# Joining the weight-times-value sets of two chunks in the fused attention stage

## Chip, cores and metric

One of the eight cores of a Trainium2 chip runs the whole kernel. The metric is the device time of one execution in microseconds, as the median of several runs. Its tensor engine is called PE here, VectorE DVE, ScalarE ACT, GpSimd POOL and SyncE SP, as in the profile.

## What is computed

The block is one transformer layer: causal attention with 16 heads of 16 columns over 8 sequences of 1024 rows, and a mixture of 8 experts, of which each row uses two, both with a residual and layer norms.

```python
q, k, v = (heads(einsum('oi,bsi->bso', W, layernorm(x))) for W in (Wq, Wk, Wv))
score = einsum('bhnd,bhmd->bhnm', q, k) / sqrt(16)        # -inf above the diagonal
out = einsum('bhnm,bhmd->bhnd', softmax(score), v)
x = x + layernorm(einsum('oi,bsi->bso', Wo, out))
logits = layernorm(x) @ router_weight.T + router_bias      # top 2 of 8 experts
x = x + layernorm(experts(layernorm(x)))
```

## The kernel before

Three stages follow one another: the fused attention stage (`attention_layer`, up to about 1412 us), the experts, and a closing sum. The change touches only the first, in which each engine runs its own unrolled list of instructions over `SLOTS`, and semaphores tie the lists together. The order within an engine is written out by hand.

**Scores and weights.** Four heads make a quad; there are 32 quads. A head has 12 *maximum* chunks (`MAXC`, here m0 to m11; widths 128, 256, 384, 512, then four times a 512 followed by 128, 256, 384, 512): PE computes scores into one of three banks `ps_s` (`max_scores`, L834) and DVE reduces them to row maxima (`maximum`, L485 and L488). The maxima pass ACT (`high`, L707) and POOL (L409), PE turns them over (`max_rows`, L841) into the third bank of `ps_s`, DVE copies them out (`mrow`, L499), and a DMA issued by POOL (L414) puts them beside the queries. m8 of the next head must wait for that copy (`c == ROWS_AT + 1`). Six heads later PE computes the scores again, now less their maximum, in 12 *exponential* chunks per quad (`EXPC`, widths 512, 384, 256, 128, four times 512, then 512, 384, 256, 128) for each of the four heads, into one of three banks `ps_e` (`exp_scores`, L853). ACT turns them into `pw` (`exponential`, L700), which holds four chunks; POOL cuts the chunks on the diagonal (L403); and `weigh` (L872) multiplies the four heads' weights with their values side by side in four column groups of 32 of the array, into one bank `ps_o`, which ACT empties twice per quad (`head_out`, L714).

**Slots.** Slot `g` stands for one exponential chunk of one quad (`NE` = 12 slots in a quad; the text numbers them 0 to 11 by `g % 12`). It has four sub-steps `s`; each holds one maximum chunk and the exponential scores of head `s` of chunk `g + 1`. The maximum of a head takes three slots, m0 to m3, m4 to m7, m8 to m11, starting at slots 0, 3, 6 and 9. `max_rows` falls into sub-step 3 of slots 1, 4, 7 and 10. At the end of each slot stands `weigh(g - 1)`. The maximum scores run from slot -18 (`BEGIN`) to 365, the exponentials for slots 0 to 383.

**Pieces between.** For each of 32 pairs of row tiles the projections for a later sequence (starts `A_AT`) and the output projection, layer norms and router of an earlier one (starts `C_AT`) are cut into pieces, each due at an offset from its start: `turn_over` (L885), `q_or_k` (L904, four steps for m = 0 and four for m = 1), `values` (L919), `project` (L944), `turn_rows` (L965), `route` (L976), `rank` (L988, L991), all through one shared bank `ps_w`: each first waits until the last user of the bank has been read (`bank_free`). Readers are on ACT `first_part` (L724), `second_part` (L730), the copies to `xn_t` (L751), `vout` (L767), `y` (L784), `h_t` (L806) and the normalisations to `xn`, `y`, `h` (L776, L789, L798); on DVE `remainder` (L508), the statistics (L593, L600, L607, L641, L650), `logits`, `top`, `top_at` (L655, L613, L619), `choose` and `place`; on POOL `third` (L394), the small row statistics (L438 to L444), the residual sum (L452) and the indirect stores of rows for the experts (L462, 128 of them at slots `S_AT`). SP issues loads and stores. The last four pairs (`LATE`) and the last groups run in slots from 384 on, without scores beside them.

## Time and profile before

| | us |
|---|---|
| median of three runs (lowest, highest) | 2316.2 (2313.4, 2321.1) |
| the profiled execution | 2312.5 |
| its span, first to last instruction | 2310.7 |
| busy in the span: PE, DVE, ACT, POOL | 2003.9, 1687.1, 1132.6, 975.5 |
| steady part of the fused stage | 200 to 1280 |
| first and last weight-times-value set | 137.8, 1320.9 |
| last indirect store for the experts begins about | 1411 |

Busy times overlap from engine to engine. A matmul's end in the profile is modelled, so neighbouring matmuls overlap on paper; the distance from start to start is what one of them keeps PE from the next. "Idle before, releaser" is the time for which an engine stood still and what ended it.

### The profile page before, as it was taken

To read this page: it belongs to the slowest core of one execution; us is meant where nothing else is said; L and a number is where in the kernel's file an instruction comes from. 1 tells how busy PE (TensorE), PEld (TensorE's weight loads), DVE (VectorE), ACT (ScalarE), POOL (GpSimd) and SP (SyncE) were. 2 spreads that over 40 slices of the span, in tenths; PEclk is the share of its full clock that TensorE was granted. 3 is DMA by queue.
4 is the path that set the end of the run, shared out by engine and by line. 5 is a ranking of instruction groups with operands and counts; after the bars stand their busy time and mean duration, and the time that the engine had idled before them with its cause. 6 is when DMAs were issued, how large, how long until landed. Compare 5 with 4: busy or idle time off the path is not lost. (4 is left out here: it accounts for less than half of the span.)

```text
span 2310.7 us, 51852 instructions
## 1 busy us (share of the span) xinstructions
PE 2003.9 (87%) x13629; PEld 1307.3 (57%) x13630; DVE 1687.1 (73%) x5978; ACT 1132.6 (49%) x2647; POOL 975.5 (42%) x1583
## 2 busy tenths in 40 slices
PE   5499999999999999999989842999999999999960
PEld 4243444444444444444333331998898888888950
DVE  2487768787888888888868232777777777777768
ACT  3156667777777777777766720222222222222220
POOL 4122334445646465555544553333333333333326
PEclk9789999999999999999999955999999999999985
DMA  5926575767666666768584223887787778778766
GB/s 156 183 63 145 125 167 150 183 153 178 146 167 140 163 145 168 152 154 172 111 215 95 97 82 136 238 242 233 238 239 236 236 233 235 232 238 238 236 193 237
DMA packets 259627, 412.94 MB, mean 179 GB/s; under 512 B 37136, under 2 KB 194960, under 8 KB 253200
## 3 DMA queue, kind: packets, MB, share of 16 engines
q1 hardware_dynamic: 220432, 367.20, 58.6%
q0 software_dynamic: 29824, 35.54, 7.4%
q10 hardware_dynamic: 9216, 8.39, 1.1%
q8 instruction: 66, 1.08, 0.2%
q14 instruction: 89, 0.73, 0.1%
HBM read 288.30 MB, written 122.14 MB: 178 GB/s over the span
## 5 line engine op out<-in xcount | busy, mean ns | idle before, releaser
L700 ACT ACTIVATE pw<-ps_e 128x512 f32<-128x512 f32 (+3 forms) x1536 | 688.7, 493 | 310.2 <-PE ps_e L853 301.7
L1244 PE MATMUL ps_g<-x_t,w_gu 128*128 128x128 f32 x4384 | 541.7, 277 | 28.1 <-ACT x_t L1175 21.9
L834 PE MATMUL ps_s<-ks,qs 96*128 96x512 bf16 (+3 forms) x1536 | 492.9, 336 | 67.0 <-DVE mrow L499 34.1
L1244 PEld LDWEIGHTS ps_g<-x_t,w_gu 128*128 128x128 f32 x4384 | 515.2, 192 | 59.2 <-issue 49.1
L485 DVE CUSTOM_DVE_ANT_0 summed<-ps_s,c 128x128 bf16<-128x128 f32 (+3 forms) x1024 | 480.3, 482 | 83.2 <-PE ps_s L834 79.4
L853 PE MATMUL ps_e<-qs,ks 98*128 98x512 bf16 (+3 forms) x1536 | 487.1, 331 | 3.2 <-ACT pw L700 3.0
L488 DVE TENSOR_REDUCE cmax<-ps_s 128x1 f32<-128x512 f32 x512 | 351.5, 686 | 142.7 <-PE ps_s L834 139.9
L834 PEld LDWEIGHTS ps_s<-ks,qs 96*128 96x128 bf16 x1536 | 152.8, 101 | 405.0 <-issue 120.2
L872 PE MATMUL ps_o<-pw,vs 128*32 128x512 f32 (+3 forms) x3072 | 332.7, 506 | 4.9 <-ACT ot L714 2.8
L1196 ACT ACTIVATE d_y<-biased,weight 128x256 f32<-128x256 f32 x136 | 69.1, 508 | 490.3 <-DVE biased L1155 490.3
L403 POOL TENSOR_SCALAR_AFFINE_SELECT pw<-pw 128x512 f32<-128x512 f32 x256 | 162.1, 633 | 310.9 <-ACT pw L700 310.8
L1210 POOL DMA_INDIRECT acc<-d_y,place_now x136 | 214.8, 1580 | 120.5 <-issue 74.5
L1273 PE MATMUL ps_y<-space,act_h 128*128 x1088 | 258.1, 380 | 0.8 <-DVE act_h L1148 0.8
L1136 DVE TENSOR_SCALAR gate<-ps_g,space 128x128 f32<-128x128 f32 x548 | 154.4, 345 | 105.4 <-issue 94.1
L853 PEld LDWEIGHTS ps_e<-qs,ks 98*128 98x128 bf16 x1536 | 149.8, 98 | 110.2 <-ACT pw L700 19.9
L1273 PEld LDWEIGHTS ps_y<-space,act_h 128*128 128x128 f32 x1088 | 196.1, 190 | 22.6 <-issue 1.5
L1203 POOL TENSOR_TENSOR place_now<-place,c 128x1 int32<-128x1 int32 x136 | 24.9, 183 | 430.9 <-ACT d_y L1196 430.5
L1141 DVE TENSOR_SCALAR up<-ps_g,space 128x128 f32<-128x128 f32 x548 | 154.3, 344 | 9.0 <-PE ps_g L1244 0.2
L462 POOL DMA_INDIRECT xs<-c_h,slot_i x128 | 131.5, 1027 | 33.2 <-issue 32.6
L872 PEld LDWEIGHTS ps_o<-pw,vs 128*32 128x32 f32 x3072 | 60.9, 108 | 121.9 <-issue 80.1
L414 POOL DMA_DIRECT2D qs<-mrow x128 | 81.5, 637 | 109.6 <-DVE mrow L499 105.3
L1179 ACT ACTIVATE sig<-gate 128x512 f32<-128x512 f32 x137 | 86.3, 630 | 79.2 <-DVE gate L1136 79.2
(136 smaller groups left out, 2289.6 us busy)
## 6 DMA issues: line engine op xcount, KB each, us to landing
w_gu<-in_gate_up SPq DMA_DIRECT2D x138, 1024.0 KB, 5.0
qk_parts<-space SPq DMA_DIRECT2D x128, 192.0 KB, 7.2
qs<-qk_parts SPq DMA_DIRECT2D x192, 128.0 KB, 7.3
ks<-qk_parts SPq DMA_DIRECT2D x192, 128.0 KB, 7.8
d_xin<-xs SPq DMA_DIRECT2D x139, 130.5 KB, 2.5
v_aug<-space SPq DMA_DIRECT2D x32, 512.0 KB, 7.4
vs<-v_aug SPq DMA_DIRECT2D x32, 512.0 KB, 11.6
o_t<-ot SPq DMA_DIRECT2D x64, 256.0 KB, 2.8
```

Of the source, the lines that this page charges most:

```text
L403: pool.affine_select(diagonal, diagonal, [[0, 4], [1, P]], ALU.is_ge, 0.0, base=0, channel_multiplier=-1).then_inc(cut_done, 1)
L485: dve.tensor_tensor_reduce(summed[:, m % RJ, 0:w], ps_s[:, m % RS, 0:w], after[:, HALF - w:HALF], 1.0, LOWEST, ALU.add, ALU.max, dst).then ...
L488: dve.reduce_max(dst, ps_s[:, m % RS, 0:w], AX.X).then_inc(s_cmax, 1)
L700: act.activation(pw[:, n % RP, 0:w], ps_e[:, n % RE, 0:w], ACT.Exp, scale=SCALE).then_inc(e_done, 1)
L834: pe.matmul(ps_s[:, m % RS, 0:w], qs[0:ROWS, slot, i * P:(i + 1) * P], ks[0:ROWS, slot, k0:k0 + w], start=True, stop=True).then_inc(s_scor ...
L853: pe.matmul(ps_e[:, n % RE, 0:w], ks[0:ROWS_M, slot, j * P:(j + 1) * P], qs[0:ROWS_M, slot, q0:q0 + w], start=True, stop=True).then_inc(e_ ...
L872: last = pe.matmul(ps_o[s * QUAD:(s + 1) * QUAD, at:at + w], vs[:, u, j, s], pw[:, (g * 4 + s) % RP, 0:w], start=(j == 0), stop=(c + 1 in ...
L1136: last = dve.tensor_scalar(gate[:, u, m], ps_g[:, u, 0, m], b_gu[:, bass.ds(e, 1), m], LIMIT, ALU.add, ALU.min)
L1141: last = dve.tensor_scalar(up[:, m], ps_g[:, u, 1, m], b_gu[:, bass.ds(e, 1), KI + m], LIMIT + 1, ALU.add, ALU.min)
L1210: pool.indirect_dma_start(out=acc, out_offset=bass.IndirectOffsetOnAxis(place_now[:, u:u + 1], 0), in_=y[:, u], in_offset=None, compute_op ...
L1244: last = pe.matmul(ps_g[:, u, half, m % KI], w_gu[:, u, k, m * P:(m + 1) * P], x_t[:, u, k], start=(k == 0), stop=(k == KT - 1))
L1273: last = pe.matmul(ps_y[:, u, 0:D], act_h[:, u, m], w_dn[:, bass.ds(e, 1), m], start=(m == 0), stop=(m == KI - 1))
```

## The change

The call of `weigh` leaves the odd slots; in each even slot `g` the sets of chunks `g - 2` and `g - 1` run one behind the other. The large PE pieces go to the odd slots: `turn_over` to slot 7, `q_or_k` m = 0 to 9, m = 1 to 11 with its last step at the head of slot 0, both `values` to 1, both halves of `project` to 3, both of `route` to 5; `turn_rows` goes to slot 4 and `rank` to slot 10. So `A_AT` moves by one slot, the readers on ACT, DVE and POOL get new offsets, `turn_rows`, `route` and what follows them run eleven slots later for the pairs before `LATE`, and the indirect stores are spread anew. No operation is added or dropped. The blocks below follow in the order SP, POOL, DVE, ACT, PE.

```diff
-    A_AT = [BEGIN - 18 + 3 * a for a in range(EARLY)] + [BEGIN - 5, BEGIN + 2] + [NE * (a - 6) - 4 for a in range(6, PAIRS)]
+    A_AT = [BEGIN - 18 + 3 * a for a in range(EARLY)] + [BEGIN - 6, BEGIN + 1] + [NE * (a - 6) - 5 for a in range(6, PAIRS)]
...
-    EVEN = [30 + d for turn in range(0, 4 * NE, NE) for d in (turn, turn + 6, turn + 7, turn + 9, turn + 10)]
+    EVEN = [34 + turn + d for turn in range(0, 3 * NE, NE) for d in (0, 3, 5, 5, 7, 9)]
...
-    MOMENTS = [(r, k) for slot, k, r in sorted((C_AT[r] + 3 + 6 * k, k, r) for r in range(PAIRS) for k in range(2))]
+    MOMENTS = [(r, k) for slot, k, r in sorted((C_AT[r] + 3 + (7 if r < LATE else 6) * k, k, r) for r in range(PAIRS) for k in range(2))]
...
+    def rows_due(steady, late, slot):
+        return [r for r, start in enumerate(C_AT) if start + (steady if r < LATE else late) == slot]
...
+    NEVER = SLOTS.stop + NE * QUADS
...
-                for a in pairs_due(-1, -9, g):
+                for a in pairs_due(-1, -8, g):
...
-                for k, offset in enumerate((5, 10)):
-                    for r in due(C_AT, offset, g):
+                for k, offsets in enumerate(((4, 4), (11, 10))):
+                    for r in rows_due(*offsets, g):
...
-                for r in due(C_AT, 7, g):
+                for r in due(C_AT, 6, g):
...
-                for a in due(A_AT, 6, g):
+                for a in pairs_due(7, 8, g):
...
-                for a in due(A_AT, 3, g):
+                for a in due(A_AT, 4, g):
...
-                        for n in groups_due(19, 19, g):
-                            choose(n, 0)
+                        for n in groups_due(31, 20, g):
+                            choose(n, 2)
                     if s == 1:
-                        for n in groups_due(22, 19, g):
-                            choose(n, 1)
-                        for n in groups_due(27, 21, g):
-                            place(n, 0)
...
+                        for a in due(A_AT, 3, g):
+                            remainder(a, 0)
...
-                        for r in due(C_AT, 9, g):
+                        for r in rows_due(10, 9, g):
...
-                        for r in due(C_AT, 17, g):
-                            half, t = r // PER % 2, r % PER * 2
-                            dve.wait_ge(c_lg, r + 1)
-                            for c in range(t, t + 2):
-                                last = dve.max(top[:, half, c], logits[:, half, c])
-                            last.then_inc(c_top, 1)
-                        for r in due(C_AT, 18, g):
+                        for r in rows_due(30, 18, g):
...
                     if s == 2:
-                        for n in groups_due(25, 19, g):
-                            choose(n, 2)
-                        for n in groups_due(27, 21, g):
+                        for n in groups_due(30, 19, g):
+                            choose(n, 0)
+                        for n in groups_due(32, 21, g):
...
-                        for n in groups_due(28, 21, g):
+                        for n in groups_due(33, 21, g):
...
-                        for n in groups_due(29, 21, g):
...
                     if s == 3:
-                        for a in due(A_AT, 2, g):
-                            remainder(a, 0)
-                        for a in due(A_AT, 4, g):
+                        for a in due(A_AT, 5, g):
...
-                        for k, offset in enumerate((4, 9)):
-                            for r in due(C_AT, offset, g):
+                        for k, offsets in enumerate(((3, 3), (10, 9))):
+                            for r in rows_due(*offsets, g):
...
-                        for r in due(C_AT, 16, g):
+                        for r in rows_due(26, 16, g):
...
+                        for r in rows_due(27, 17, g):
+                            half, t = r // PER % 2, r % PER * 2
+                            dve.wait_ge(c_lg, r + 1)
+                            for c in range(t, t + 2):
+                                last = dve.max(top[:, half, c], logits[:, half, c])
+                            last.then_inc(c_top, 1)
+                        for n in groups_due(30, 19, g):
+                            choose(n, 1)
+                        for n in groups_due(31, 20, g):
+                            place(n, 0)
...
                     if s == 2:
-                        for a in due(A_AT, 0, g):
-                            act.wait_ge(a_tps, a + 1)
-                            if a >= 2:
-                                act.wait_ge(a_v, a - 1)
-                            bank = ps_e[:, 0] if a < EARLY else ps_w[:]
-                            act.activation(xn_t[:, a % 2], bank.rearrange("p (k t) -> p k t", k=KT), ACT.Copy).then_inc(a_xt, 1)
-                        for a in due(A_AT, 2, g):
-                            first_part(a, 0)
-                        for a in due(A_AT, 3, g):
-                            second_part(a, 0)
-                        for a in due(A_AT, 4, g):
-                            first_part(a, 1)
-                        for a in due(A_AT, 5, g):
-                            second_part(a, 1)
-                        for a in due(A_AT, 6, g):
+                        for a in due(A_AT, 7, g):
...
-                        for a in pairs_due(-2, -10, g):
+                        for a in due(A_AT, 0, g):
+                            act.wait_ge(a_tps, a + 1)
+                            if a >= 2:
+                                act.wait_ge(a_v, a - 1)
+                            bank = ps_e[:, 0] if a < EARLY else ps_w[:]
+                            act.activation(xn_t[:, a % 2], bank.rearrange("p (k t) -> p k t", k=KT), ACT.Copy).then_inc(a_xt, 1)
+                        for a in due(A_AT, 6, g):
+                            second_part(a, 1)
+                        for a in due(A_AT, 3, g):
+                            second_part(a, 0)
+                        for a in due(A_AT, 5, g):
+                            first_part(a, 1)
+                        for a in pairs_due(-2, -9, g):
...
-                        for r in due(C_AT, 1, g):
-                            bank = ps_w[:] if r < LATE else ps_s[:, r % 2]
-                            act.wait_ge(c_w, r + 1)
-                            if r >= 2:
-                                act.wait_ge(c_x1, r - 1)
-                            act.activation(y[:, r % 2], w_view(bank), ACT.Copy).then_inc(c_raw, 1)
-                        for r in due(C_AT, 6, g):
+                        for r in due(C_AT, 5, g):
...
-                        for r in due(C_AT, 11, g):
+                        for r in rows_due(15, 11, g):
...
-                        for r in due(C_AT, 14, g):
+                        for r in rows_due(25, 14, g):
...
-                        for n in groups_due(20, 20, g):
+                        for n in groups_due(31, 20, g):
...
+                    if s == 3:
+                        for a in due(A_AT, 2, g):
+                            first_part(a, 0)
+                        for r in rows_due(0, 1, g):
+                            bank = ps_w[:] if r < LATE else ps_s[:, r % 2]
+                            act.wait_ge(c_w, r + 1)
+                            if r >= 2:
+                                act.wait_ge(c_x1, r - 1)
+                            act.activation(y[:, r % 2], w_view(bank), ACT.Copy).then_inc(c_raw, 1)
...
                     if s == 0:
-                        for n in groups_due(27, 20, g):
+                        for a in due(A_AT, 5, g):
+                            q_or_k(a, 1, (3,))
+                        for n in groups_due(NEVER, 20, g):
...
-                        for a in due(A_AT, 4, g):
-                            q_or_k(a, 1, (1,))
                     if s == 1:
...
-                        for a in due(A_AT, 1, g):
+                        for a in due(A_AT, 2, g):
...
+                        for a in due(A_AT, 4, g):
+                            q_or_k(a, 1, (0, 1))
+                        for a in due(A_AT, 6, g):
+                            values(a, 0)
+                        for r in due(C_AT, 0, g):
+                            project(r, 0)
+                        for r in rows_due(25, 14, g):
+                            turn_rows(r)
+                        for r in rows_due(26, 16, g):
+                            route(r, 0)
+                            route(r, 1)
+                    if s == 2:
...
-                            q_or_k(a, 1, (2, 3))
-                        for a in due(A_AT, 5, g):
-                            values(a, 0)
+                            q_or_k(a, 1, (2,))
...
-                            project(r, 0)
-                        for r in due(C_AT, 1, g):
...
-                        for r in due(C_AT, 14, g):
-                            turn_rows(r)
-                        for r in due(C_AT, 16, g):
-                            route(r, 1)
-                    if s == 2:
-                        for a in due(A_AT, 3, g):
-                            q_or_k(a, 1, (0,))
-                        for r in due(C_AT, 15, g):
-                            route(r, 0)
-                if 0 < g <= NE * QUADS:
-                    weigh(g - 1)
+                        for n in groups_due(31, NEVER, g):
+                            rank(n)
+                if g % 2 == 0:
+                    for chunk in (g - 2, g - 1):
+                        if 0 <= chunk < NE * QUADS:
+                            weigh(chunk)
```

## Rows read from the trace of the kernel before

**Rows 1.** The page, busy time, share of the span and instructions of PE.
```profile
PE 2003.9 (87%) x13629; PEld 1307.3 (57%) x13630; DVE 1687.1 (73%) x5978; ACT 1132.6 (49%) x2647; POOL 975.5 (42%) x1583
```
**Rows 2.** Windows, steady stretch: length, busy PE, PEld, DVE, ACT, POOL, clock, DMA, GB/s.
```profile
200.00:1280.00 1080.00, 1030.05 (x6837) 479.00 (x6837) 855.04 (x3158) 795.60 (x1920) 532.19 (x939) 0.99 0.66 154
```
**Rows 3.** Groups by shape, PE, 200 to 1280 us: busy, mean ns | idle before, releasers.
```profile
L834 PE MATMUL ps_s<-ks,qs 96*128 96x512 bf16 x687 | 262.6, 386 | 30.8 <-DVE mrow L499 22.0 <-DVE rmax L485 7.6 <-DVE cmax L488 1.1
...
L872 PE MATMUL ps_o<-pw,vs 128*32 128x512 f32 x1352 | 185.0, 620 | 1.9 <-ACT ot L714 1.3
...
L919 PE MATMUL ps_w<-space 128*128 128x256 f32 x192 | 53.1, 399 | 10.8 <-DVE space L508 10.8
...
L976 PE MATMUL ps_w<-w_r,h_t 128*128 128x8 f32 x200 | 25.8, 237 | 2.1 <-DVE base L548 2.1
```
**Rows 4.** Timeline of PE, slots 11 to 1: start, duration, instruction, count.
```profile
704.37 0.38 PE L834 MATMUL ps_s<-ks,qs 96*128 96x512 bf16 x1
704.59 0.38 PE L853 MATMUL ps_e<-qs,ks 98*128 98x512 bf16 x1
704.90 0.64 PE L872 MATMUL ps_o<-pw,vs 128*32 128x256 f32 x8
705.47 0.23 PE L834 MATMUL ps_s<-ks,qs 96*128 96x128 bf16 x1
...
708.08 0.43 PE L872 MATMUL ps_o<-pw,vs 128*32 128x128 f32 x8
708.44 0.39 PE L834 MATMUL ps_s<-ks,qs 96*128 96x512 bf16 x1
...
709.56 1.13 PE L919 MATMUL ps_w<-space 128*128 128x256 f32 x4 [0.45 <-DVE space L508]
```
**Rows 5.** Timeline of PE, last slots of the stage: two sets in one group.
```profile
1318.70 1.28 PE L872 MATMUL ps_o<-pw,vs 128*32 128x384 f32 x16
```
**Rows 6.** Timeline of all engines, slot 0: the chain ahead of the values.
```profile
707.44 0.33 PE L853 MATMUL ps_e<-qs,ks 98*128 98x384 bf16 x1
...
707.81 0.49 ACT L700 ACTIVATE pw<-ps_e 128x384 f32<-128x384 f32 x1 [0.71 <-PE ps_e L853]
...
708.19 0.59 ACT L724 ACTIVATE space<-ps_w 128x512 bf16<-128x512 f32 x1
...
708.82 0.69 DVE L508 TENSOR_TENSOR space<-ps_w,space 128x512 f32<-128x512 f32 x1
```
**Rows 7.** Windows, four us behind a long wait for mrow (columns as rows 2).
```profile
222.00:226.00 4.00, 4.00 (x16) 0.88 (x15) 2.02 (x8) 1.94 (x4) 1.21 (x4) 0.50 0.69 268
```
**Rows 8.** Timeline, transpose of the maxima and its copy, slot 1, then slot 7.
```profile
711.07 0.22 PE L841 MATMUL ps_s<-c,mpart 128*16 128x128 bf16 x1
...
711.56 0.20 DVE L499 COPY mrow<-ps_s 16x128 bf16<-16x128 bf16 x1
...
729.86 0.22 PE L841 MATMUL ps_s<-c,mpart 128*16 128x128 bf16 x1
730.25 0.20 DVE L499 COPY mrow<-ps_s 16x128 bf16<-16x128 bf16 x1
```
**Rows 9.** Timeline, slots 4 and 5: the copy and the m8 that waits for it.
```profile
721.57 0.21 DVE L499 COPY mrow<-ps_s 16x128 bf16<-16x128 bf16 x1 [0.62 <-DMA qs<-mrow]
...
721.93 0.38 PE L834 MATMUL ps_s<-ks,qs 96*128 96x512 bf16 x1 [0.55 <-DVE mrow L499]
```
**Rows 10.** Timeline of ACT, slot 3: two exponentials of 512 columns.
```profile
718.96 1.08 ACT L700 ACTIVATE pw<-ps_e 128x512 f32<-128x512 f32 x2 [0.42 <-PE ps_e L853]
```
**Rows 11.** Timeline of PE and DVE, slot 10 of a late quad: m4 and m7.
```profile
1111.02 0.39 PE L834 MATMUL ps_s<-ks,qs 96*128 96x512 bf16 x1
...
1111.45 0.69 DVE L488 TENSOR_REDUCE cmax<-ps_s 128x1 f32<-128x512 f32 x1
...
1112.19 0.28 PE L834 MATMUL ps_s<-ks,qs 96*128 96x256 bf16 x1 [0.25 <-DVE cmax L488]
```
**Rows 12.** Groups of POOL, 1371 to 1412 us.
```profile
L462 POOL DMA_INDIRECT xs<-c_h,slot_i x31 | 30.6, 987 | 9.6 <-issue 9.6
```

## The prediction

> **What bounds the kernel now.** The tensor engine (PE) leads over the span [rows 1]. I read next the table of stages: in the steady stretch of the fused stage, 200 to 1280 us, PE is busy 1030 of 1080 us at granted clock 0.99, VectorE (DVE) 855 and ScalarE (ACT) 796 [rows 2]. Then the PE groups by shape in the same stretch: the reader is to see how little PE idles. The maximum scores wait 30.8 us (22.0 of it for the copy of mrow), the values products 10.8, the weight-times-value sets 1.9, the router product 2.1 [rows 3]. So PE's own time counts there, and a change is worth what it takes from PE's queue less what it makes PE wait for. A chunk slot lasts about 3.1 us; I number the twelve slots of a quad 0 to 11, and the twelve maximum scores of a head m0 to m11. Last I read PE's timeline from start to start, since modelled ends overlap.
>
> **Part by part. 1, the sets joined.** Scores follow a 512-wide score after 0.22 us, a set only after 0.31: 0.09, here taken as 0.10, lies ahead of a set. A set of 256 columns holds PE 0.57 us, one of 128 columns 0.36: 0.21 per 128 columns and 0.15 that doesn't depend on width [rows 4]. Two sets back to back occur once in the trace, in the last slots: 384 and 256 columns, modelled 1.28 us together [rows 5]; apart they would take 0.21 x 3 + 0.15 and then 0.64 (the duration of the lone 256-column set), 1.42. So joining saves 0.14 behind one set and 0.10 ahead of the next, 0.245 per pair. The maximum scores end at slot 366 and PE is the bound until then: 183 pairs, **-45 us**. Lower bound: only the front gap, -18.
>
> The Trainium skill, "TensorE: Matmul & The Clock Gate", Part 3 (Packing small matmuls), says that a weight load overlaps running matmuls only when it goes to other row groups; the weights of both sets use all rows, so by it the second set could not start seamlessly and only the -18 would be left. The joined pair speaks against it [rows 5]; it is rival 4.
>
> **2, the values products.** They now start 0.45 us late by the record, 0.6 from start to start, because the remainder of the projection ends just before [rows 4, 6]. Afterwards the last query/key piece runs at the head of slot 0, and the four scores' rest (about 1.0), a weigh pair of 128+256 columns (0.9) and 0.5 of slot 1 lie between: 2.4 us. The chain it waits for: exponential 0.37 behind its matmul, 0.38 to the next activation, first part 0.6, remainder 0.7 [rows 6], started 0.43 late: 2.6. Left 0.24 of 0.62, 28 times: **-11** (0 to -17).
>
> **3, the waits for ot and base** [rows 3] get a slot more or a weigh pair in front: with the slack around them **-5**.
>
> **4, the mrow copy.** In slot 4 DVE waits for the DMA of the previous mrow, and m8 of the next slot waits for the copy; PE idles 22.0 us in all [rows 3]. The path of the DMA stays; what lies between on PE grows from a 128-column set to 384 columns in a pair (+0.4), and part 6's wait comes ahead of it. I take 13 of the 22. Around the longest of these waits the clock falls to half for a few us [rows 7]; four such places before 360 us cost about 2 us each; I give back 2: **-15** (0 to -30).
>
> **5, the same copy where no set covers it.** The mrow transpose is the last but one matmul of slots 1, 4, 7 and 10, and m8, first in the next slot, waits for the copy out of PSUM. Transpose to copy is 0.49 us in slot 1 and 0.39 in slot 7 [rows 8]; copy to m8, where nothing else holds PE, is 0.36 [rows 9]. Now a set always lies between. Afterwards the sets are in even slots, so behind slots 1 and 7 only one exponential score does: 0.15 + 0.11 and 0.15 + 0.22. PE waits 0.85 - 0.26 = 0.59 and 0.75 - 0.37 = 0.38: 0.97 a quad, 31 quads, **+30** (+15 if the copy comes quicker, +35). Queued behind m8 is everything of PE; DVE and ACT run dry meanwhile.
>
> **6, turning of rows.** project moves whole into slot 3, y's copy to slot 3 behind its last exponential and the small high part (0.2), and turn_rows of an earlier pair needs that PSUM bank in slot 4, sub-step 1. From project's end: exponential score 0.22, 0.37 to ACT [rows 6], 0.48 for the exponential (two in 1.08 us) [rows 10], 0.2, copy and signal 0.65: 1.9 us. PE has 1.16 of scores. Wait 0.75, 26 pairs: **+19** (+5 if ACT lets the copy pass sooner, +30 if it lags). The old place had a set and more than a slot between.
>
> **7, rank** moves to slot 10, sub-step 2, and needs the bank that the remainder in sub-step 1 reads, itself behind a first part at the end of slot 9: by the chain of part 2 about 1 us, for six groups, **+6**.
>
> **8, DVE's pace.** PE may be three maximum banks ahead. Where four maxima follow without other PE work, the fourth waits for the first. Trace of slot 10 in a late quad, without pieces: m4 issued at 1111.02, DVE starts it 0.43 later, needs 0.69, m7 goes at 1112.19 where PE was ready 0.4 earlier [rows 11]. Afterwards slots 2, 6, 8, 10 are without pieces in every quad. Slot 10: m3 (512 wide, DVE 0.6) now lies 0.33 ahead of m4, with no set between, so m4 ends at 1.4 and m7, wanted at 0.68, waits 0.8. Slot 2: m8 ends at 1.2, m11 wanted at 0.78: 0.4. Slot 6: m2 waits for m11 behind slot 5's 2.6 us of DVE work, 0.3. Sum 1.5. The trace's own small waits of this kind, 0.45 a quad in PE's start-to-start excess, go: +1.05, 30 quads, **+31** (0 if DVE runs no later than now, +50).
>
> **9, outside.** Head: the same pieces, values and vout one slot later; stores still at +9: +1 (-3 to +5). The last 18 slots, where ACT sets the pace with exponentials: wider breaks, +2. Tail: POOL's 31 indirect stores run to its end at 1.3 us each [rows 12]; what starts them is the last pair's chain, which gets pair 27's turning, router and y copy in front (about 2 us), and one more store stays behind it (1.3): +3. Together **+6** (-3 to +12). SP's queue keeps its order but for the input load, one slot later and not near a wait; POOL's third and row statistics move by a slot under its idle time. Both at nothing, +3 if DVE then waits for them.
>
> **Sum.** -45 - 11 - 5 - 15 + 30 + 19 + 6 + 31 + 6 = +16. The profiled execution took 2312.5 us (span 2310.7 and 1.8 around it), the median of three runs 3.7 more. 2312.5 + 16 = 2328.5; half of the 3.7 added, **2330**.
>
> **Rivals.** 1, not slower: DVE's pace does not bite. It stays ahead because PE's new waits (5, 6) let it catch up; then term 8 is zero and 6 falls by 5: 16 - 31 - 5 = -20, 2294 with the same half; with the lower bounds of 5 and 6 it reaches 2270. For it: DVE is busy only 79% [rows 2]. Against: the late wait came with DVE just as idle [rows 11]. It decides at the point where m4 is done within 0.7 us of its issue in slot 10. 2, the costs of 5 and 6 hold and half of 8: all cancels, 2309 to 2323. 3, slower by more: ACT starves in the joined sets. A pair of two 512-column sets holds PE 1.95 us, three banked exponentials last 1.45 [rows 10]; 0.5 and 0.4 of latency idle ACT. In slots 5 and 6 ACT's work is 5.5 us (eight exponentials, ot, the high part, h's two normalisations that move there) against PE's 5.8, so 0.6 is over, in 7 and 8 0.2: +24, 2354. Against it: the normalisations lie just ahead of the sets and count as bank. 4, the joined set does not start seamlessly: 27 of the 45 are lost, 2357.
>
> **Chances.** Forecast (2323 to 2345) 0.41, rival 1 0.30, rival 2 0.17, rival 3 0.07, rival 4 0.05. Measurement tells 0.3%, 7 us. Slower 0.41 + 0.07 + 0.05 = 0.53; same 0.17; faster 0.30. The range cuts the low third of rival 1 and the tops of 3 and 4: 2282 to 2352. Signs are mixed, so the forecast's own 2323 to 2345 stands beside it.
>
> **What would show it.** Right: weigh groups of 16 records whose time is 0.21 per 128 columns + 0.15 once; PE's wait for mrow above 22 us, at slots 2 and 8, with about 0.6 and 0.4 each; a PE wait for y's copy before turn_rows of 0.5 to 1; no 0.45 before the values; maximum scores in slots 2, 6, 10 waiting for cmax. Wrong: PE idle in the stretch not above the 45 us it has now, or DVE and ACT waiting for PE more while PE has no gaps (rival 1); ACT without waits and PE waiting for pw (rival 3); a joined group as long as two (rival 4). What would make the forecast wrong is above all the size of 8, an addition over several slots.

## The result, and the profile after

| | before | after |
|---|---|---|
| median of four runs each (lowest, highest) | 2314.8 (2310.1, 2321.1) | 2355.7 (2352.9, 2365.0) |
| span of the profiled execution | 2310.7 | 2355.7 |

The changed kernel is slower: ratio 1.0182, 95% interval 1.0144 to 1.022, some 41 us by the medians and 45 by the profiled spans. The forecast, 2330 with a range of 2282 to 2352, had the sign and 14 us of it. Among the experiments below only one run (3580.2 us, of before_light2) fell into a slower state; it is left out of that kernel's median.

The page's busy times of after (PE, its loads, DVE, ACT, POOL), and the row of the steady stretch, which answers to [rows 2]:

```profile
PE 2011.2 (85%) x13629; PEld 1331.0 (57%) x13630; DVE 1687.2 (72%) x5978; ACT 1132.4 (48%) x2647; POOL 972.4 (41%) x1583
...
200.00:1280.00 1080.00, 1001.97 (x6628) 486.16 (x6621) 825.14 (x3041) 770.50 (x1859) 513.14 (x912) 0.98 0.66 152
```

PE was busy for 1030 us of this stretch and is for 1002, 2.7% less; DVE and ACT, whose work per quad is unchanged, are busy for 3.5% and 3.2% less. So the same time holds some 3.3% less of the kernel's work, and PE's gain can't be read from this row: its busy time per quad did not fall, since it holds part of the waits and the slower clock. The distances from start to start below show it. The groups of PE by shape, 200 to 1280 us (busy, mean ns | idle before, releasers), answer to [rows 3]:

```profile
L839 PE MATMUL ps_s<-ks,qs 96*128 96x512 bf16 x663 | 255.4, 387 | 40.6 <-DVE mrow L504 18.1 <-DVE rmax L490 16.3 <-DVE cmax L493 6.0
L858 PE MATMUL ps_e<-qs,ks 98*128 98x512 bf16 x660 | 243.9, 384 | 1.3 <-ACT pw L704 1.2
L877 PE MATMUL ps_o<-pw,vs 128*32 128x512 f32 x1324 | 171.5, 621 | 0.0
...
L924 PE MATMUL ps_w<-space 128*128 128x256 f32 x192 | 51.8, 392 | 5.5 <-DVE space L513 4.0
```

The maximum scores wait 40.6 us in place of 30.8, and DVE's maxima (L490, L493) hold most of what is new. Two waits did not exist before, for y's copy ahead of `turn_rows` (L970) and for the remainder ahead of `rank` (L993); a view of PE's waits in the same stretch (waited for: us in total, times, longest) lists them:

```profile
PE ps_s L839 <- DVE mrow L504: 18.1, 61, 1.5
...
PE ps_w L970 <- ACT c_y L817: 13.4, 24, 0.6
PE ps_s L839 <- DVE cmax L493: 10.0, 51, 0.3
PE ps_w L993 <- DVE space L513: 7.4, 4, 1.8
PE ps_w L924 <- DVE space L513: 4.0, 4, 1.0
```

Mrow's wait fell from 22.0 to 18.1 us, but it came in 21 places and comes in 61.

**Where the 45 us lie.** From the start of the first maximum score of a slot to the same of a later slot, in both timelines:

| stretch | before | after | difference |
|---|---|---|---|
| start to slot 0 | 131.9 | 137.5 | +5.6 |
| quads 0 and 1 | 71.8 | 72.8 | +1.0 |
| quads 2 to 5 | 160.2 | 149.9 | -10.3 |
| quads 6 to 23 | 678.4 | 707.0 | +28.6 |
| quads 24 to 29 | 221.8 | 235.0 | +13.3 |
| slot 360 to the last set | 56.9 | 62.7 | +5.7 |
| from there to the end | 989.8 | 990.8 | +1.0 |

Windows over the same stretches give the granted clock (third number from the end). Before, then after:

```profile
203.70:363.90 160.20, 150.16 (x928) 65.61 (x924) 115.31 (x399) 108.12 (x262) 54.64 (x104) 0.93 0.64 147
363.90:1042.30 678.40, 658.89 (x4433) 321.02 (x4430) 550.34 (x2046) 517.43 (x1248) 360.91 (x635) 1.00 0.68 160
1042.30:1264.00 221.70, 202.17 (x1360) 84.30 (x1356) 172.70 (x660) 154.03 (x374) 105.86 (x182) 0.98 0.67 151
```

```profile
210.30:360.20 149.90, 139.58 (x913) 65.14 (x912) 113.16 (x391) 106.54 (x260) 54.56 (x104) 1.00 0.68 158
360.20:1067.20 707.00, 663.27 (x4430) 333.59 (x4428) 550.91 (x2045) 519.54 (x1246) 359.84 (x636) 0.99 0.66 153
1067.20:1302.20 235.00, 209.31 (x1353) 89.97 (x1352) 171.12 (x650) 152.88 (x373) 102.21 (x179) 0.93 0.63 141
```

In quads 2 to 5 the low clock of [rows 7] is gone (0.93, now 1.00), and with it 10 us. How much of this belongs to the change isn't sure: late_turn and rank_turn, below, run the same code in these quads and take 148.8 us at 1.00 and 156.9 at 0.96. In quads 24 to 29 the opposite happened (0.98, now 0.93): PE idles 25.7 us in place of 19.5 and is busy 7.1 us longer with less to do.

**The joined set itself.** PE's timeline in slots 0 to 2 of quad 12 (start, duration, instruction, count):

```profile
596.29 0.86 PE L877 MATMUL ps_o<-pw,vs 128*32 128x256 f32 x16
597.08 0.39 PE L839 MATMUL ps_s<-ks,qs 96*128 96x512 bf16 x1
...
600.19 0.22 PE L846 MATMUL ps_s<-c,mpart 128*16 128x128 bf16 x1
600.35 0.28 PE L858 MATMUL ps_e<-qs,ks 98*128 98x256 bf16 x1
600.81 0.38 PE L839 MATMUL ps_s<-ks,qs 96*128 96x512 bf16 x1 [0.18 <-DVE mrow L504]
...
601.97 0.39 PE L839 MATMUL ps_s<-ks,qs 96*128 96x512 bf16 x1 [0.23 <-DVE cmax L493]
602.20 0.22 PE L858 MATMUL ps_e<-qs,ks 98*128 98x128 bf16 x1
602.35 1.71 PE L877 MATMUL ps_o<-pw,vs 128*32 128x512 f32 x16
603.99 0.23 PE L839 MATMUL ps_s<-ks,qs 96*128 96x128 bf16 x1
```

Sets of 256 and 128 columns together keep PE 597.08 - 596.29 = 0.79 us (0.57 + 0.36 apart, [rows 4]); those of 512 and 384 take 603.99 - 602.35 = 1.64. The second set starts seamlessly. After 600.81 and ahead of 601.97 one sees the two kinds of wait that the set in the odd slot used to cover.

### The profile page after: what moved, and what is told of

It is laid out like the page before. It is cut to its first block and busy times, and to the rows that moved or that the text cites. A ratio compares the mean times of both kernels' runs of the same rounds, so it can differ in the third digit from the quotient of the medians.

```text
span 2355.7 us, 51852 instructions
## 1 busy us (share of the span) xinstructions
PE 2011.2 (85%) x13629; PEld 1331.0 (57%) x13630; DVE 1687.2 (72%) x5978; ACT 1132.4 (48%) x2647; POOL 972.4 (41%) x1583
## 5 line engine op out<-in xcount | busy, mean ns | idle before, releaser
L839 PE MATMUL ps_s<-ks,qs 96*128 96x512 bf16 (+3 forms) x1536 | 498.8, 336 | 87.6 <-DVE mrow L504 28.3
L490 DVE CUSTOM_DVE_ANT_0 summed<-ps_s,c 128x128 bf16<-128x128 f32 (+3 forms) x1024 | 480.4, 482 | 125.0 <-PE ps_s L839 121.5
L493 DVE TENSOR_REDUCE cmax<-ps_s 128x1 f32<-128x512 f32 x512 | 352.3, 688 | 147.0 <-PE ps_s L839 134.0
L877 PE MATMUL ps_o<-pw,vs 128*32 128x512 f32 (+3 forms) x3072 | 301.4, 511 | 0.2 <-POOL pw L408 0.2
L877 PEld LDWEIGHTS ps_o<-pw,vs 128*32 128x32 f32 x3072 | 82.0, 111 | 146.2 <-issue 96.5
L909 PE MATMUL ps_w<-space 128*128 128x256 f32 x448 | 124.6, 392 | 6.6 <-DVE space L513 4.0
```

What stands on the lines that cost most here:

```text
L490: dve.tensor_tensor_reduce(summed[:, m % RJ, 0:w], ps_s[:, m % RS, 0:w], after[:, HALF - w:HALF], 1.0, LOWEST, ALU.add, ALU.max, dst).then ...
L493: dve.reduce_max(dst, ps_s[:, m % RS, 0:w], AX.X).then_inc(s_cmax, 1)
L839: pe.matmul(ps_s[:, m % RS, 0:w], qs[0:ROWS, slot, i * P:(i + 1) * P], ks[0:ROWS, slot, k0:k0 + w], start=True, stop=True).then_inc(s_scor ...
L877: last = pe.matmul(ps_o[s * QUAD:(s + 1) * QUAD, at:at + w], vs[:, u, j, s], pw[:, (g * 4 + s) % RP, 0:w], start=(j == 0), stop=(c + 1 in ...
```

## The experiments

Each ratio is to runs of the kernel before on the same chip. "Ordinary quad" is the mean of the same fourteen quads of every kernel, 6 to 23 without 9, 13, 17 and 21 (which hold a rank, but for the three kernels that move it a quad further), from start to start; "late" is slot 288 to slot 360, quads 24 to 29. Both come from one profiled run of each kernel. Two pairs of kernels with the same code in quads 6 to 23 (after and late_apart, rank_turn and rank_turn_apart) differ there by 3 us.

| kernel | median (us) | ratio, 95% interval | ordinary quad | late |
|---|---|---|---|---|
| before | 2314.8 | | 37.56 | 221.8 |
| after | 2355.7 | 1.0182 (1.0144 to 1.022) | 38.61 | 235.0 |
| join_only | 2327.6 | 1.0056 (1.0035 to 1.0077) | 37.88 | 227.4 |
| moves_only | 2337.6 | 1.0099 (1.006 to 1.0138) | 38.53 | 225.8 |
| early_copy | 2355.4 | 1.0169 (1.0124 to 1.0215) | 38.97 | 234.7 |
| late_turn | 2348.4 | 1.0146 (1.0106 to 1.0186) | 38.44 | 235.4 |
| rank_covered | 2342.6 | 1.0162 (1.011 to 1.0214) | 38.36 | 229.3 |
| after_light | 2329.7 | 1.0083 (1.0054 to 1.0111) | 38.01 | 226.1 |
| before_light | 2303.0 | 0.9986 (0.9967 to 1.0006) | 37.28 | 221.3 |
| join_third | 2329.1 | 1.0098 (1.0065 to 1.0131) | 38.34 | 227.7 |
| join_two | 2300.0 | 0.995 (0.9933 to 0.9968) | 37.40 | 219.1 |
| join_zero | 2302.6 | 0.9964 (0.9947 to 0.9982) | 37.55 | 222.8 |
| before_light2 | 2286.0 | 0.9905 (0.9875 to 0.9934) | 37.22 | 222.7 |
| join_light2 | 2283.8 | 0.9878 (0.9857 to 0.99) | 36.91 | 217.7 |
| late_apart | 2340.1 | 1.0117 (1.0084 to 1.015) | 38.60 | 228.1 |
| rank_turn | 2335.9 | 1.0101 (1.0074 to 1.0127) | 38.13 | 225.1 |
| rank_turn_apart | 2326.5 | 1.006 (1.0033 to 1.0088) | 38.26 | 220.1 |

The kernel before took 2314.9 us on the chip of the first four experiments (join_only to late_turn), 2307.3 on that of the next four, 2311.3 on the third and 2314.4 on the last, so ratios compare and bare medians do so only within a group.

**The two halves of the change.** join_only is the kernel before with the new call; moves_only is the changed kernel with the old one.

```diff
-                if 0 < g <= NE * QUADS:
-                    weigh(g - 1)
+                if g % 2 == 0:
+                    for chunk in (g - 2, g - 1):
+                        if 0 <= chunk < NE * QUADS:
+                            weigh(chunk)
```

> The kernel before with only the call of weigh changed (sets of two chunks in even slots); no piece moves. Theory A (the joined set pays 0.245 us a pair and the loss comes from waits that the moved pieces lay open): per middle quad -1.5 for the join, +0.7 for the mrow copy in slots 1 and 7, -0.4 for the values, -0.4 for mrow in slot 4: about -1.6 a quad and no clock drops before 360 us, so 2262 (2250 to 2275), clearly faster than before. Theory B (the joined sets themselves starve ScalarE and VectorE, wherever the pieces lie): 2335 or more.

> The changed kernel with the old call of weigh: a set at the end of each slot, pieces at their new places. Theory A: a set now lies again behind every slot, so the mrow copy in slots 1 and 7 and most of y's copy in slot 4 are covered and slot 10 waits 0.2 instead of 0.9; only the join's gain is missing: 2312 (2300 to 2325), near the kernel before. Theory B: near before too. A third theory, that the moved pieces cost as much without the join: 2345 and more.

Theory A, that joining is worth its PE time, missed join_only by over 60 us: the joined kernel is 0.56% slower than before, though not by as much as theory B had asked for (2335 or more). The moves cost 1.0% by themselves, 2337.6 us, where A had at most 2325 and the third theory at least 2345. In an ordinary quad nearly all of the change's loss is there with the moves alone (38.53 us, 38.61 with the join on top): the moved pieces leave slots 2 and 10 to DVE's pace, with waits of 0.39 and 0.60 us although a set still stands in every slot. Of the 14.6 us by which the profiled span of after exceeds that of moves_only, 7.3 lie in the quads 9, 13, 17 and 21 with a rank, 9.2 in the late quads and 1.1 in the ordinary ones. Join_only's groups (200 to 1280 us) and, from its timeline, slot 6 of a quad show who is late:

```profile
L834 PE MATMUL ps_s<-ks,qs 96*128 96x512 bf16 x683 | 258.2, 383 | 40.9 <-DVE mrow L499 31.5 <-DVE rmax L485 7.6 <-DVE cmax L488 1.1
L853 PE MATMUL ps_e<-qs,ks 98*128 98x512 bf16 x682 | 252.5, 385 | 11.1 <-ACT pw L700 9.1
```

```profile
526.28 0.60 ACT L714 ACTIVATE ot<-ps_o 128x512 f32<-128x512 f32 x1
...
527.23 0.63 ACT L806 ACTIVATE h_t<-ps_w 128x512 f32<-128x512 f32 x1
527.71 2.11 ACT L700 ACTIVATE pw<-ps_e 128x512 f32<-128x512 f32 x4
```

```profile
527.65 0.33 PE L834 MATMUL ps_s<-ks,qs 96*128 96x384 bf16 x1
528.41 0.39 PE L853 MATMUL ps_e<-qs,ks 98*128 98x512 bf16 x1 [0.43 <-ACT pw L700]
```

Mrow takes 31.5 us of PE in place of 22.0 (the copies of slots 1 and 7 lie bare, 0.57 and 0.37 us an ordinary quad), and in slots 5 and 6, which hold eight exponentials of 512 columns, ACT has the copies to ot and h_t to do as well; PE's next score of the exponential waits 0.85 us a quad for a bank. In the kernel before, the set of slot 5 stood there. That is rival 3's mechanism, in a kernel without the moves; in the changed one ACT holds PE for only 1.3 us in this group, so the moves mended it.

**early_copy and late_turn** aim at two waits of the changed kernel.

```diff
-    ROWS_AT, HIGH_AT = 7, 3
+    ROWS_AT, HIGH_AT = 6, 3
```

> The changed kernel, with the mrow transpose one sub-step earlier (sub-step 2 of slots 1, 4, 7, 10), so that m7 and its exponential score lie between the copy and m8. Theory A: the two waits of 0.35 in slots 1 and 7 and about 1 us of the late quads' slot 1 go: 2330 (2322 to 2338). Theory B: no more than 5 us change. If VectorE's wait for the transpose takes the place, also no change.

```diff
+                    if s == 3:
+                        for r in rows_due(25, 14, g):
+                            turn_rows(r)
```

(Taken out of sub-step 1; its reader on ACT goes to sub-step 3 as well.)

> The changed kernel, with turn_rows and its reader h_t in sub-step 3 of slot 4 in place of sub-steps 1 and 2, so that two more maxima and exponential scores lie between y's copy and it. Theory A: the wait of 0.72 us in slot 4 goes 26 times: 2337 (2331 to 2345). Theory B: no change.

early_copy changed nothing (theory A, 2330, missed; what the expectation's last sentence says came). In its groups the mrow wait ahead of m8 shrank from 18.1 to 6.4 us, but the transpose, which takes the bank of m5 and must wait until DVE has read it, comes a sub-step sooner and now waits itself:

```profile
L846 PE MATMUL ps_s<-c,mpart 128*16 128x128 bf16 x111 | 24.6, 222 | 23.7 <-DVE cmax L490 23.7
```

The changed kernel has 0.4 us there. late_turn took away the 13.4 us for y's copy and returned 0.36%, some 8 us, less than its theory A had asked for (2331 to 2345) and within the two intervals; in the trace an ordinary quad is 0.17 us shorter. The wait became waits of 0.1 to 0.2 us for DVE and mrow in the same slot.

**rank_covered** puts the rank of the first six groups into slot 8. In the changed kernel it stands in slot 10; PE there, then DVE and a window over the joined set:

```profile
665.33 0.22 PE L858 MATMUL ps_e<-qs,ks 98*128 98x128 bf16 x1
667.39 0.21 PE L993 MATMUL ps_w<-sel,c 128*128 128x72 bf16 x1 [1.85 <-DVE space L513]
...
668.16 2.82 PE L877 MATMUL ps_o<-pw,vs 128*32 128x512 f32 x16
```

```profile
664.96 0.83 DVE L533 TENSOR_TENSOR hot<-c,at_f 128x64 f32<-128x64 f32 x2
...
666.32 0.21 DVE L538 TENSOR_TENSOR sel<-hot 128x64 bf16<-128x64 f32 x1
...
666.66 0.68 DVE L513 TENSOR_TENSOR space<-ps_w,space 128x512 f32<-128x512 f32 x1
```

```profile
669.00:671.00 2.00, 2.00 (x13) 0.31 (x6) 0.00 (x0) 0.29 (x2) 1.62 (x3) 0.50 0.28 75
```

Ahead of the rank DVE works off, behind m3, the comparisons (`hot`) and the sum (`sel`) of `choose`, which the change puts there, with m4 and m5 between, and only then the remainder.

```diff
-                        for n in groups_due(31, NEVER, g):
+                        for n in ranks_due(41, 31, NEVER, g):
                             rank(n)
```

(`place` and the stores of these groups go ten slots later too.)

> The changed kernel, with the rank of the first six groups ten slots later: in slot 8 of a quad, where a transposed pair and a query/key piece lie around it and no remainder of the projection has its PSUM bank, in place of slot 10. Theory R (the rank waits 1.85 to 2.01 us for the remainder, and after it the joined set runs at a granted clock of 0.50 for 3.4 us; together 3.5 us in a quad with a rank, about six of them): both go, the quads 9, 13, 17 and 21 fall from 41.7 to about 38.5 us, the median from 2355 to 2334 to 2340. Rival: the half clock belongs to the rank itself and not to the wait, and comes along to the new place; then only the 2 us of the wait go, six times, 2343 to 2345, and the windows of low clock lie ten slots later.

In slot 8 the rank waits for nothing and the clock stays up:

```profile
694.04 0.20 PE L997 MATMUL ps_w<-sel,c 128*128 128x72 bf16 x1
...
694.76 1.92 PE L881 MATMUL ps_o<-pw,vs 128*32 128x512 f32 x16
```

```profile
693.90:697.90 4.00, 4.00 (x38) 1.92 (x38) 3.33 (x18) 3.04 (x8) 2.71 (x4) 1.00 0.03 5
```

(The set here is of two 512-wide chunks; that of slot 10 is of 512 and 384 columns, 1.71 us by its record when undisturbed, so it lost 1.1 us.) So the half clock doesn't belong to the rank (the rival falls). It doesn't follow from the wait each time either: late_apart, below, has the changed kernel's code in quad 9, and there the same wait is followed by full clock:

```profile
510.14 0.21 PE L993 MATMUL ps_w<-sel,c 128*128 128x72 bf16 x1 [1.84 <-DVE space L513]
...
510.90 1.71 PE L877 MATMUL ps_o<-pw,vs 128*32 128x512 f32 x16
```

```profile
510.10:514.10 4.00, 3.96 (x36) 2.07 (x37) 2.56 (x9) 2.77 (x7) 1.97 (x3) 1.00 0.95 365
```

Half clock followed this wait four times of four in after, three of four in late_turn and two of four in late_apart. A rank quad of after with it takes 41.7 us, one of late_apart without it 40.05, so the half clock costs 1.6 us a time.

In rank_covered the quads 9, 13, 17 and 21 that have lost their rank take 39.08 us in place of 41.62, those that have it now 38.4, and the last set starts at 1345.5, 19 us earlier. From there to the end it is 995.3 us in place of 990.8, so 15 of the 19 reach the span (rank_turn's expectation, below, says 21 and 6 longer, counted to an earlier set). The later stores were meant to be harmless: 41 of them now stand behind the last set in place of 36, and the last begins 91.6 us behind it in place of 89.9; the rest is in the experts, which take from 882.2 to 887.5 us in the seventeen profiles with the same code there. In rank_turn against late_turn the last store begins 94.4 in place of 86.5 us behind the last set, so there the later stores do cost. The 15 us are of one profile on a chip that runs the kernel before 7.5 us quicker; in ratios the gain is 0.2%, some 5 us, not clear of noise and short of the 15 to 21 expected. rank_turn against late_turn, below, gives 0.45%.

**Lighter maxima.** One edit on either kernel:

```diff
-                    dve.reduce_max(dst, ps_s[:, m % RS, 0:w], AX.X).then_inc(s_cmax, 1)
+                    dve.reduce_max(dst, ps_s[:, m % RS, 0:w // 2], AX.X).then_inc(s_cmax, 1)
```

> The changed kernel with the maximum taken over half the columns in the six of twelve chunks (m4, m6, m8, m10 and the halves of m5 and m7 by their width) that VectorE reduces without a mask; it leaves out half of those columns from the row maxima. PE's work is the same. Theory D (in slots 2, 6 and 10 PE waits for VectorE's pace, 1.5 us a quad): the wait of 0.40 in slot 2 goes, of the 0.88 in slot 10 about 0.4 goes (m6 there waits for m3, which keeps its width), and mrow comes a little sooner, 0.1 at each place; 0.9 x 28 = 25, about 2330. Rival (these waits are latency from one engine to the other, not VectorE's work): within 5 us of the changed kernel, 2350 to 2356.

> The kernel before with the same lighter maxima (it leaves out half of the columns of the unmasked chunks from the row maxima). Theory D: VectorE sets little here, only the small waits of 0.3 us in all and part of those for mrow in slot 4: 2305 to 2312. The distance between the two light kernels is then about 20, where between the full ones it is 41. Rival (latency only): 2312 to 2315 and a distance of still 40.

(It concerns four chunks of a head, m4, m6, m8 and m10; the number six in the expectation was a slip.) The changed kernel gains 1.0%, 23 us, the one before 0.3%, 6 us, at most: the distance falls from 1.8% to 1.0%. So close to half of it is DVE's pace, by taking DVE's work and nothing else. Against the light kernel before, the light changed one loses 2.4 us ahead of slot 0 and 4.8 in the late quads, where the full kernels differ by 5.6 and 13.3. An ordinary quad of the changed kernel loses 0.60 us, in slot 2 (0.40 to 0.14), slot 10 (0.88 to 0.65), slot 6 and slot 7, and gets 0.16 back in slot 4.

**join_third** keeps a set in every slot that has an mrow transpose and joins four pairs.

```diff
+                if g % 3 != 2:
+                    for chunk in (g - 2, g - 1) if g % 3 == 0 else (g - 1,):
```

> The kernel before with four pairs of sets joined in a quad in place of six: those of slots 2 and 3, 5 and 6, 8 and 9, 11 and 0 stand in the second slot of each, and the four slots with an mrow transpose (1, 4, 7, 10) keep a set of their own. Theory B (in the kernel with all pairs joined the 1.5 us that a quad gains were eaten by mrow copies without cover in slots 1 and 7, 0.94 us a quad, by exponentials that came late in slot 6, 0.85, and by the transpose in slot 10, 0.5): the first and the last of these can't come, the second can: 0.98 - 0.8 = 0.2 a quad, 2305 to 2312. Theory C (what ate the gain was the mrow copy alone, the rest would come back as soon as it is covered): 4 x 0.245 x 30 = 29, 2286. Theory E (a joined set starves ScalarE wherever it stands, 0.2 us for each pair or more): 2315 or above.

Theory E is what happened, 1.0% slower. Mrow is no longer bare in slots 1 and 7, but each slot that lost its set hands the bill to the next one. Its groups:

```profile
L853 PE MATMUL ps_e<-qs,ks 98*128 98x512 bf16 x676 | 253.5, 387 | 10.5 <-ACT pw L700 8.7
...
L834 PE MATMUL ps_s<-ks,qs 96*128 96x256 bf16 x226 | 62.9, 279 | 12.1 <-DVE cmax L488 9.1
```

Slot 2 without a set lasts 1.98 us, in which DVE gets four maxima of 0.55 to 0.69 each; slots 3 and 9 start with waits of 0.33 and 0.29 for DVE, slot 6 waits 0.8 for ACT. Only slots 11 and 0 stayed free of new waits, and there the values' wait fell from 0.62 to 0.17.

**join_two and join_zero** follow from that: join only where the slots show no new wait.

```diff
+                if g % NE not in (3, 11):
+                    for chunk in (g - 2, g - 1) if g % NE in (4, 0) else (g - 1,):
```

(join_zero: `(11,)` and `(0,)`.)

> The kernel before with two pairs of sets joined in a quad: chunks 10 and 11 in slot 0, chunks 2 and 3 in slot 4; every other set stays where it was. From the per-slot times of the kernels with six and with four pairs: in slots 11 and 0 the joined pair met no new wait, and the wait for the values ahead of the products in slot 1 fell from 0.62 to 0.17 us; in slots 3 and 4 the wait for mrow fell from 0.6 to 0.42. Theory E' (joining pays where the slot left without a set isn't followed by work that VectorE or ScalarE has to hurry for): 2 x 0.245 + 0.3 + 0.1 = 0.9 us a quad, 27 us, and for what comes late elsewhere some of it back: 2288 to 2304 where the kernel before takes 2314. Theory E (a joined set starves the other engines wherever it stands): 2314 or above.

> The kernel before with one pair of sets joined in a quad, chunks 10 and 11 in slot 0. Theory E': 0.245 + 0.3 (values) = 0.55 us a quad, 16 us, 2298 to 2306 where the kernel before takes 2314. Theory E: 2314 or above.

Both are faster than the kernel before, by less than 1%: 0.995 (0.9933 to 0.9968), 11 us, and 0.9964 (0.9947 to 0.9982), 8 us. That is 11 of 27 us and half of 16 that the sums promised; both lie at the upper end of the times that theory E' gave. The groups of join_two in the stretch:

```profile
L834 PE MATMUL ps_s<-ks,qs 96*128 96x512 bf16 x686 | 264.6, 389 | 37.7 <-DVE mrow L499 31.1 <-DVE rmax L485 4.5 <-DVE cmax L488 1.1
...
L919 PE MATMUL ps_w<-space 128*128 128x256 f32 x192 | 53.1, 399 | 0.6 <-DVE space L508 0.2
```

The values' 10.8 us are 0.6 now; mrow's 22.0 are 31.1. PE reaches slot 4 sooner and waits there for the DMA of the previous mrow, whose path is no shorter (0.60 to 0.91 us a quad); with join_zero it is 0.89. A gain ahead of a latency-bound wait is given back at it.

**Is the joined set itself at fault?** The last pair lightens ACT as well:

```diff
-                act.activation(pw[:, n % RP, 0:w], ps_e[:, n % RE, 0:w], ACT.Exp, scale=SCALE).then_inc(e_done, 1)
+                act.activation(pw[:, n % RP, 0:max(P, w // 2)], ps_e[:, n % RE, 0:max(P, w // 2)], ACT.Exp, scale=SCALE).then_inc(e_done, 1)
```

> The kernel before with VectorE's unmasked maxima over half their columns and ScalarE's exponentials over half theirs (at least 128); it leaves out half of the columns of both, so its weights are not the reference's. PE's work is unchanged. It is the base for the kernel with all pairs joined and the same two cuts. All theories: PE sets its time as before, 2295 to 2308 where the kernel before takes 2314 (some of the waits for mrow and the values go).

> The kernel with all pairs joined and nothing moved, with the same two cuts (half the columns of the unmasked maxima and of the exponentials are left out). Theory P (joining the sets saves its 1.5 us a quad, and what eats it is the pace of ScalarE and VectorE between two sets, with three PSUM banks each to run on, and the mrow copies without cover): the first goes with the cuts, the second stays with 0.8 us a quad, so 0.5 to 0.7 us a quad is gained on the other light kernel, 15 to 20 us, where the full kernels stand at 12 us the other way. Theory C' (the joined sets themselves cost PE time, by the clock or by the order of loads): the distance stays, 5 to 15 us slower than the other light kernel.

(In both, DVE also fills `pw` once with a constant, so that the columns left out hold numbers.) Joining all six pairs, 0.56% slower with full work on ACT and DVE, is not slower with light work: 2286.0 and 2283.8 us, a difference of 0.1% in medians and 0.3% in the ratios, with intervals that overlap and profiled spans of 2284.2 and 2284.8. So no gain of the whole kernel is shown; that is clear of theory C', which had asked for 5 to 15 us more, and far from the 15 to 20 of theory P. The quads show the sign: 6 to 29 take 894.8 us and joined 884.8, with full work 900.1 and joined 914.7. From slot 360 to the last set 5 us are given back. So the joined set costs PE nothing of itself in the quads, and most of what eats its gain there is the pace of the engines around it.

**late_apart, rank_turn, rank_turn_apart** ask for the last quads and for additivity. With `QUADS` = 32 the bound `NE * (QUADS - 6)` is slot 312, not 288 as the expectations say: the sets stand apart only from quad 26 on, and quads 24 and 25 keep the joined ones.

```diff
-                if g % 2 == 0:
+                if g % 2 == 0 and g <= NE * (QUADS - 6):
...
+                elif NE * (QUADS - 6) < g <= NE * QUADS:
+                    weigh(g - 1)
```

> The changed kernel with the sets of the last six quads (24 to 29, chunks from 288 on) one to a slot again; in these quads nothing of the projections of rows is left that fills the odd slots. They took 235.0 us from slot 288 to slot 360 in the changed kernel, 221.7 in the one before and 225.8 with all moves and no join. Theory L (in these quads the joined sets cost, in place of saving: PE empties its three banks in the slot without a set, the copy of mrow lies bare, and at the half granted clock that follows the long set takes 0.5 to 0.9 us longer): the stretch falls to about 226, the median by 8 to 10, 2345 where the changed kernel takes 2355. Rival (the late quads are slower by the moves alone): within 3 us of the changed kernel.

> The changed kernel with two of its waits taken away at once: the rank of the first six groups in slot 8 in place of 10, and turn_rows at the end of slot 4. Apart they brought some 10 (the last weight set 21 us earlier, but what follows it 6 us longer) and 7 us. If the two are independent and the time behind the last weight set is scatter: 2355 - 15 - 7 = 2333, 1.008 of the kernel before. Rival (what one gives back is lost at the next wait): 2342 or more, 1.012.

> Both of these and the sets of the last six quads one to a slot. Theories of the two runs before hold and add up: 2333 - 9 = 2324, 1.004 of the kernel before; what is left of the distance are the waits of the slots 1, 2, 6, 7 and 10, 1 us a quad in quads 6 to 23, 18 us, less the four windows of half clock ahead of 360 us that are gone, 10 us. Rival: 1.010 or more.

late_apart: slots 288 to 360 take 228.1 us in place of 235.0, the kernel 0.65% less, 15 us. Of these, 5.5 lie in quads 26 to 29 (152.7 in place of 158.2) and 2.9 between slot 360 and the last set; 4.7 lie ahead of slot 312, where the two kernels are the same (scatter, 3.0 of it in the quads 9 and 21, which here kept full clock), and the rest behind. rank_turn_apart against rank_turn gives the same: 4.3 in quads 26 to 29 and 3.9 behind slot 360. So the joined sets cost 8 us from quad 26 on, and the rival falls. But they are not all of it: with the joined sets kept and the ranks moved, slots 288 to 360 take 229.3 us (rank_covered) and 225.1 (rank_turn), with lighter maxima 226.1. In a late quad of the changed kernel:

```profile
1268.96 0.38 PE L839 MATMUL ps_s<-ks,qs 96*128 96x512 bf16 x1 [0.94 <-DVE mrow L504]
...
1270.77 2.68 PE L877 MATMUL ps_o<-pw,vs 128*32 128x512 f32 x16
```

```profile
1270.00:1273.00 3.00, 3.00 (x20) 0.73 (x18) 1.91 (x7) 0.59 (x3) 1.57 (x4) 0.54 0.94 131
```

Without pieces slot 1 is 2.8 us long, the copy of mrow is bare for 0.94 of it, and the joined set, PE's longest work, falls into the half clock that follows: 2.68 us in place of 1.71. (Low clock alone is not the price: moves_only has 0.94 in these quads, after 0.93, and takes 225.8 us.) rank_turn (1.0101) gains 0.8% on the changed kernel, between its theory (1.008) and the rival (1.012), and rank_turn_apart 1.2% (1.006, with 1.004 and 1.010 expected), where late_turn, rank_covered and late_apart alone gave 0.36, 0.20 and 0.65: within their intervals they add up. What is left of 1.0182 is 0.6%, 14 us.

## Why the prediction was right or wrong

The sign and most mechanisms were right, the time was not. What failed is step 7 (the rank), which left out two terms, the size of step 8 (DVE's pace), and the sum itself, which took the late quads for ordinary ones.

The working is checked against the mean of the fourteen ordinary quads. PE's wait at a place is the distance from start to start less that of undisturbed pairs of the same kind:

| step, us a quad | forecast | measured |
|---|---|---|
| 1, join of six pairs | -1.47 | -1.41 |
| 2, values (0.62 before) | -0.38 | -0.12 |
| 3, ot | -0.17 | -0.09 |
| 4, mrow in slot 4 | -0.5 | -0.55 |
| 5, mrow bare in slots 1 and 7 | +0.97 | +0.71 |
| 6, y's copy | +0.75 | +0.72 |
| 8, DVE's pace | +1.05 | +1.66 |
| sum | +0.25 | +0.92 (quad: +1.05) |

**Step 1 held.** Per pair of 512 columns, 2 x 1.00 + 0.09 apart and 1.86 joined, 0.23 against 0.245. Rival 4, which gave nearly the measured time (2357), falls; of the rule in the Trainium skill, "TensorE: Matmul & The Clock Gate", Part 3 (Packing small matmuls), that a weight load overlaps running matmuls only in other row groups, the trace shows no cost here: all sixteen go through at the pace of one set.

**Step 2 was too hopeful**: the values wait 0.50, not 0.24. In moves_only, with the old sets, it is 0.82, so it was the moved pieces that made it worse and the joined set that gave back. **Steps 4 to 6 held within 0.3**, y's wait within 0.03 (the record shows 0.56 of it, 24 times). But late_turn and early_copy show that each covered a next wait: 19 us of step 6 are worth 8.

**Step 8 had the mechanism and too small a size.** Forecast 1.5 in slots 2, 6 and 10, less 0.45 of old small waits; measured 0.40 + 0.41 + 0.07 + 0.88 = 1.76 in slots 2, 6, 8, 10, and only 0.1 of old waits went. So of the 0.61 that the step was short, 0.35 is the credit for old waits and only 0.26 the new ones. Together with step 2 and less what the others were too high, this makes 0.8 us a quad over what was forecast, 14 us in quads 6 to 23. after_light supports the cause: half the columns in four maxima take 0.6 us of it. The waits of slots 2 and 10 come with the moved pieces more than with the join (0.39 and 0.60 in moves_only), that of slot 6 with the join. Rival 1 is refuted at its own deciding point: it wanted DVE to be done with m4 within 0.7 us of its issue in slot 10, where m7, which waits for that, starts 1.45 us behind it, and PE waits 0.88 in all.

**Step 7 was the step that failed in kind**: 1 us a rank was counted. Two terms were left out. DVE's queue ahead of the remainder holds the comparisons and the sum of `choose`, 0.83 and 0.21 us, that the change puts there, so the wait is 1.85 by the record and 2.01 from start to start; and behind it the granted clock was 0.50 in all four of these quads, while PE holds its longest work, the joined set: 2.82 us in place of 1.71. With what follows that makes 2.4 us more than in the kernel before, four times in quads 6 to 23. Moving the ranks gives 5 us by the ratios of rank_covered and 10 by rank_turn against late_turn, where 6 were forecast; only the quads' lengths settle the 2.4.

**What was not asked.** The sum treated all 30 quads alike. The last six have few or no pieces in the odd slots, so what a set had covered lies bare for longer, and joined sets fall into low clock: +13.3 us, where the forecast's surplus of an ordinary quad makes 1.5 and the measured one 6.3. The joined sets account for about 5 of it (late_apart); moving the ranks takes 6 to 10 away, and the two can overlap. This is step 9's kind of stretch, and it was given 2 us from slot 360 on (measured 5.7) and 1 at the head (measured 5.6, also in moves_only, whose slot 0 starts at 138.3, so with the moves; in after_light it starts at 132.0, so DVE's work has a part in it). In the other direction step 4 gave back 2 us for low clock; in quads 2 to 5 10.3 came, part of which may be luck of the one profile.

**Balance.** Against the forecast of +16 for the span: quads 6 to 23 +20 (14 of pace and values, 6 of ranks), late quads +12, head +5, slots from 360 and the end +2, quads 2 to 5 -9 and quads 0 and 1 near nothing: +30 of the 29 missing, within the rounding. With the end of the range at 2352 the result lay 4 us outside it. Rival 3 (2354) gave nearly the right time for a wrong reason: in the changed kernel ACT is not late. Two signs of the forecast did not come: mrow's wait is 18.1 us, not above 22, and PE still waits ahead of the values.

What stays open is how the late quads' 13.3 us divide between the joined sets, the ranks and the clock, what brings half clock behind one wait and not behind the next of the same length, and the 0.13 us a quad between the sum of the steps and the quad's length.

## What to carry to other kernels

A group of matmuls that keeps PE from asking for anything is also the time in which the engines with three banks each catch up. Moving it costs at both ends: behind the place that it leaves PE outruns DVE, and where it lands the others go dry. The pieces between do the same: moved away alone, they cost 1.0% here. So count, for each slot between two such groups, the work of every engine against PE's, queue by queue, with what else stands in it, and join only where no slot turns over (two of six pairs here, -0.5%). A wait of PE can also have the price of what runs at half clock behind it: add that price with the longest group that follows (1.6 us here, three times of four), and look at the stretches without filler work on their own.

## What the runs showed of the hardware

Sixteen matmuls, four column groups wide, with weight loads between, run as closely over the seam of two sets as inside one (1.86 us for 512 and 512 columns, 1.00 for one). A wait of 1.85 us for the remainder was followed by granted clock 0.50, the lower of the clock's two levels (1.2 in place of 2.4 GHz), in nine of twelve cases (after, late_turn, late_apart), and by 1.00 in the other three. In moves_only it is 1.28 and was followed by 1.00 four times of four, while the waits of 0.65 ahead of the ranks of quads 25 and 29 in after were followed by 0.50: the length of one wait does not tell. A wait of 0.94, with smaller ones around it, was followed by 0.54. With the wait gone (rank_covered) the rank and the set behind it ran at 1.00. I had counted such low stretches only around the longest waits for a DMA.
